# Attention's VectorE steps of the routing and of the x update in other periods, two TensorE jobs exchanged at attention's end, and one GpSimd power moved in the MLP

## The reference

```python
x = x + attn_a(layernorm(x))     # 16 heads of 64, causal softmax, output matrix W_O
x = x + ffn(layernorm(x))        # mixture of experts
x = x + attn_b(layernorm(x))     # linear attention, 8 heads, and a gated MLP
x = x + ffn(layernorm(x))        # the same mixture of experts again
```

```python
def attn_a(x):                                   # per row of x and head
    scores = tril(k @ q.T) - 1e10 * (1 - mask)
    attn = softmax(scores / 8)
    z = attn @ v;   return z_flat @ W_O.T
def ffn(x):                                      # x is normalised a second time inside
    xn = (x - mu) * rsqrt(var + eps) * gamma + beta
    probs = softmax(xn @ Wr + br)                # 8 experts
    scores, idx = top_k(probs, 2)
    full = relu(xn @ W1[e] + b1[e]) @ W2[e] + b2[e]
    return x + sum(scores * (full[idx] - c[idx] + c.sum()))
```

## Time and profile before

| | |
|---|---|
| median of 3 runs | 1351.04 us (1348.25 to 1354.89) |
| profiled execution, time | 1348.61 us |
| profiled execution, span | 1346.7 us |
| TensorE busy | 1208.7 us (90%) |
| VectorE busy | 912.4 us (68%) |
| ScalarE busy | 829.2 us (62%) |
| GpSimd busy | 505.1 us (38%) |
| attention's rows 1 to 7 | about 78 to 524 us |

### The profile page before, as it was taken

One profiled execution on the slowest core, in us unless ns is written; L12 is line 12 of the kernel. 1 busy time (PEld: TensorE's weight loads), 2 busy tenths in 40 slices (PEclk: granted clock), 3 DMA queues, 4 the chain that ended last, 5 costly groups with the idle time before them and its releaser, 6 DMA issues. The chain is left out here.

```text
span 1346.7 us, 26854 instructions
## 1 busy us (share of the span) xinstructions
PE 1208.7 (90%) x7787; PEld 917.0 (68%) x7787; DVE 912.4 (68%) x3538; ACT 829.2 (62%) x2478; POOL 505.1 (38%) x619
## 2 busy tenths in 40 slices
PE   6999999999999998799985999999996988199990
PEld 5666666666666665599973777777774656199990
DVE  6788888887878785444436888888873667234445
ACT  6898888888888886144432555656554665044440
POOL 2111324142414131545541344433432376545550
PEclk9999999999999999799996999999997999599995
DMA  9100000000000000222221000000000011222226
GB/s 291 49 2 1 12 7 11 7 13 6 16 7 13 5 13 1 72 69 71 69 64 62 17 16 17 17 1 1 1 1 0 15 39 40 76 59 73 69 71 195
DMA packets 54442, 52.89 MB, mean 39 GB/s; under 512 B 7341, under 2 KB 43098, under 8 KB 54330
## 3 DMA queue, kind: packets, MB, share of 16 engines
q1 hardware_dynamic: 36320, 29.39, 7.7%
q0 software_dynamic: 8928, 17.84, 3.9%
q10 hardware_dynamic: 9082, 4.33, 1.1%
HBM read 29.48 MB, written 22.05 MB: 38 GB/s over the span
## 5 line engine op out<-in xcount | busy, mean ns | idle before, releaser
L1354 ACT ACTIVATE prob<-prob,negmax 128x256 f32<-128x256 f32 (+3 forms) x512 | 283.2, 556 | 47.6 <-DVE negmax L1448 47.5
L1448 DVE CUSTOM_DVE_ANT_0 prob<-bank,mask 128x256 f32<-128x256 f32 (+3 forms) x512 | 223.9, 480 | 41.9 <-PE bank L1164 41.6
L1524 POOL TENSOR_TENSOR Vs<-Vh_sb,rinv 128x512 f32<-128x512 f32 x64 | 66.6, 1041 | 365.7 <-DVE rinv L1426 365.7
L1050 POOL DMA_INDIRECT expert_out<-f_x_yb,f_x_to x142 | 136.7, 963 | 153.0 <-DVE f_x_yb L1038 118.3
L1176 PE MATMUL bank<-prob,Vs 128*64 128x512 f32 (+3 forms) x1024 | 152.0, 439 | 0.5 <-POOL Vs L1524 0.4
L678 POOL DMA_INDIRECT expert_in<-f_xn,f_slot x128 | 126.9, 991 | 49.1 <-issue 31.2
L982 PE MATMUL bank<-f_x_xbT,W_sb 128*128 128x256 f32 x568 | 138.3, 387 | 1.7 <-DVE f_x_xbT L1018 1.7
L1003 ACT ACTIVATE f_x_hid<-bank,cols 128x256 f32<-128x256 f32 x144 | 63.8, 474 | 92.1 <-PE bank L982 92.1
L982 PEld LDWEIGHTS bank<-f_x_xbT,W_sb 128*128 128x128 f32 x568 | 104.6, 194 | 14.8 <-DVE f_x_xbT L1018 2.9
L1003 ACT ACTIVATE prob<-bank,cols 128x256 f32<-128x256 f32 x140 | 62.0, 473 | 79.6 <-PE bank L982 79.6
L1176 PEld LDWEIGHTS bank<-prob,Vs 128*64 128x64 f32 x1024 | 63.6, 136 | 69.7 <-issue 60.0
(11 more groups left out here) (263 smaller groups left out, 3181.2 us busy)
## 6 DMA issues: line engine op xcount, KB each, us to landing
f_x_xb<-expert_in SPq DMA_DIRECT2D x73, 130.0 KB, 2.2
b_crows<-expert_out SPq DMA_DIRECT2D x16, 256.0 KB, 2.7
c_crows<-expert_out SPq DMA_DIRECT2D x16, 256.0 KB, 4.2
expert_out<-f_x_yb,f_x_to POOLq DMA_INDIRECT x142, 2.5
expert_in<-fill ACTq DMA_DIRECT2D x16, 130.0 KB, 2.5
x_sb<-in_L_attn_a_x_dram SPq DMA_DIRECT2D x8, 256.0 KB, 6.7
W_sb<-in_L_ffn_W_dram SPq DMA_DIRECT2D x1, 2048.0 KB, 10.2
expert_in<-f_xn,f_slot POOLq DMA_INDIRECT x128, 2.3
```

Of the source, the lines that this page charges most:

```text
L1050: pool.indirect_dma_start(yg, bass.IndirectOffsetOnAxis(ap=self.to[:, t:t + 1], axis=0), self.yb[:, t, :], None).then_inc(self.stored[t], 16)
L1354: nc.scalar.activation(mine, mine, ACT.Exp, scale=-1.0, bias=negmax[:, g % 2, i, a:a + 1], accum_out=rowsum[:, g % 2, i, a:a + 1]).then_in ...
L1448: nc.vector.tensor_tensor_reduce(out=prob[:, g % 2, a, columns(i)], in0=score_bank(i, a), in1=mask[:, T - width[i]:], scale=-1.0, scalar=H ...
```

## The change

Four edits; the number of instructions on every engine stays the same.

1. The x update in place leaves `dve_normalise`, becomes `dve_update`, and in attention's rows comes behind P4 instead of behind P3. It also waits for the normalised tiles.
2. `dve_top` and `dve_topid` of the routing go from behind P6 to inside P6, after mask j = 5. The five later steps stay behind P6.
3. At attention's end `PV` of pair 7 comes ahead of `out_of` of pair 6.
4. At the MLP's end the power of row 7 comes ahead of all scatters of row 6.

```diff
-                if self.in_place and not self.lean:
-                    self.wait_rstd(dve, b, update=True)
-                    for t in range(NT):
-                        tile = self.src[:, bass.ds(b * NT + t, 1), :]
-                        nc.vector.tensor_scalar(tile, tile, self.power[:, u, 6, t:t + 1], self.power[:, u, 7, t:t + 1],
-                                                ALU.mult, ALU.subtract).then_inc(self.y, 1)
+
+            def dve_update(self, dve, b, u):
+                self.wait_rstd(dve, b, update=True)
+                dve.wait_ge(self.xn, START + b * NT + NT)
+                for t in range(NT):
...
-            ROUTE_DVE = {5: (route.dve_logit, route.dve_rmax, route.dve_shift),
-                         6: (route.dve_top, route.dve_topid, route.dve_ids,
-                             route.dve_is_k, route.dve_sel, route.dve_row_sel),
-                         7: (route.dve_place, route.dve_picked, route.dve_slotf, route.dve_slots)}
+            ROUTE_DVE_INSIDE = {5: (route.dve_logit,), 6: (route.dve_top, route.dve_topid), 7: (route.dve_place,)}
+            ROUTE_DVE_BEHIND = {5: (route.dve_rmax, route.dve_shift),
+                                6: (route.dve_ids, route.dve_is_k, route.dve_sel, route.dve_row_sel),
+                                7: (route.dve_picked, route.dve_slotf, route.dve_slots)}
...
+                    PV(B - 1, PAIRS - 1)
                     out_of(B - 1, PAIRS - 2)
-                    PV(B - 1, PAIRS - 1)
                     out_of(B - 1, PAIRS - 1)
...
-                                    if g in (ROUTE_LOGITS, ROUTE_RANK) and not first:
-                                        ROUTE_DVE[g][0](dve, b - 1, 1 - u)
+                                    if not first:
+                                        for part in ROUTE_DVE_INSIDE.get(g, ()):
+                                            part(dve, b - 1, 1 - u)
...
-                                for part in ROUTE_DVE.get(g, ()):
-                                    if part not in (route.dve_logit, route.dve_place):
-                                        part(dve, b - 1, 1 - u)
+                                if g == ROUTE_TR:
+                                    route.norm.dve_update(dve, b - 1, 1 - u)
+                                for part in ROUTE_DVE_BEHIND.get(g, ()):
+                                    part(dve, b - 1, 1 - u)
...
                     route.dve_normalise(dve, B - 1, 1)
+                    route.norm.dve_update(dve, B - 1, 1)
...
-                        route.pool_scatter(pool, LAST - 1, slot_of(LAST - 1), 0, 2)
                         route.norm.pool_power(pool, LAST, slot_of(LAST))
-                        route.pool_scatter(pool, LAST - 1, slot_of(LAST - 1), 2)
+                        route.pool_scatter(pool, LAST - 1, slot_of(LAST - 1))
                         route.pool_scatter(pool, LAST, slot_of(LAST))
```

More of the change, by code:

```diff
@@ L405, in dve_normalise @@
                                             ALU.subtract, ALU.mult).then_inc(self.xn, 1)
-                if self.in_place and not self.lean:
-                    self.wait_rstd(dve, b, update=True)
-                    for t in range(NT):
-                        tile = self.src[:, bass.ds(b * NT + t, 1), :]
-                        nc.vector.tensor_scalar(tile, tile, self.power[:, u, 6, t:t + 1], self.power[:, u, 7, t:t + 1],
-                                                ALU.mult, ALU.subtract).then_inc(self.y, 1)
+            def dve_update(self, dve, b, u):
+                self.wait_rstd(dve, b, update=True)
+                dve.wait_ge(self.xn, START + b * NT + NT)
+                for t in range(NT):
+                    tile = self.src[:, bass.ds(b * NT + t, 1), :]
+                    nc.vector.tensor_scalar(tile, tile, self.power[:, u, 6, t:t + 1], self.power[:, u, 7, t:t + 1],
+                                            ALU.mult, ALU.subtract).then_inc(self.y, 1)
             def pool_finish(self, pool, b, u):
@@ L1500, in _ @@
                     route.dve_normalise(dve, B - 1, 1)
-                    for g in ROUTE_DVE:
-                        for part in ROUTE_DVE[g]:
+                    route.norm.dve_update(dve, B - 1, 1)
+                    for g in ROUTE_DVE_INSIDE:
+                        for part in (*ROUTE_DVE_INSIDE[g], *ROUTE_DVE_BEHIND[g]):
                             part(dve, B - 1, 1)
```

## The result

| | before | after |
|---|---|---|
| median | 1351.72 us of 4 runs (1348.25 to 1354.89) | 1339.03 us of 4 runs (1338.33 to 1340.33) |
| ratio to before, 95% interval | | 0.9898 [0.9869, 0.9928] |
| profiled execution, time | 1348.61 us | 1339.15 us |
| profiled execution, span | 1346.7 us | 1336.8 us |

A forecast was written before the change was run, and what follows sets the result against it. TensorE, busy most of the span, was taken to bound the kernel, losing time to VectorE's late first masks. Terms -4.2 - 5.3 + 0.8 - 1.5 = -10.2 us gave a median of 1340.8 us, range 1335 to 1347.

The forecast's parts named there:

- The reading: Attention's P4 and P7: a late first mask on VectorE delays TensorE's small job beyond 2.92 us by the same amount.
- P4, -4.2: Moving the x update behind P4 gives back 0.62 us in six rows and 0.53 in the last: 4.2 us.
- P5's room, 0.14 us: The moved 1.02 us update fits VectorE's 1.16 us wait ahead of P5's first mask, with 0.14 us to spare.
- P7, -5.3: Moving part of the selection inside P6 lets P7's first mask start earlier: 3.4 to 5.7 us back, 5.3 taken.
- The worst case (0.27 us late): P7's first mask, after a late K_lo and five remaining steps, still starts 0.27 us late instead of 0.82.
- PV in front, +0.8: Attention's end: the exchange makes one TensorE rest of 2.8 us; range -0.5 to +1.5 us, +0.8 taken.
- The +1.5: Attention's end: if the clock falls inside PV, the statistics and all 16 scatters wait 1.5 us longer; sum then -9.5.
- The last power, -1.5: MLP's end: the power starts 1.5 us earlier, and row 7's slots and scatters follow 1.5 us earlier.
- The K_lo wait: Rival: K_lo of P6 becomes 1.23 us late and delays P7, so P7 returns nothing: 1346.1 us, chance 0.14.
- The clock did not stay up: Rival at attention's end: the clock stays up in PV, -0.5 instead of +0.8: 1339.5 us, chance 0.27.
- VectorE's wait ahead of P5 is no free time: Rival: moved work is paid wherever put, P5 7.1 and P6 8.6 us: +5.8 in all, 1356.8 us, chance 0.04.
- The change did what it says: Opposed rival: attention's waits are really ScalarE's pace and periods stay as long; 1350.3 us, chance 0.07.

The follow-up runs named there:

- edits 2, 3 and 4 alone: Three kernels, each the kernel before with only edit 2, only edit 3 or only edit 4: 1345.13, 1352.64 and 1350.59 us.
- edit 3 alone: The kernel before with only PV of pair 7 put ahead of out_of of pair 6 at attention's end: 1352.64 us, ratio 0.9997.
- edit 4 alone: The kernel before with only the MLP's last power put ahead of all scatters of row 6: 1350.59 us, ratio 0.9991.
- the rest filled: Changed kernel with ten unread matmuls in TensorE's rest ahead of the last value product: 1338.91 us; with due work there and six scatters moved earlier: 1336.04 us.
- the kernel with two sums: The changed kernel with two unused VectorE sums over 128x512 behind the x update in P4: 1352.2 us, ratio 0.9999.
- edit 1 alone: The kernel before with only the x update moved from behind P3 to behind P4: 1348.97 us, ratio 0.9967.
- the doses: The changed kernel with two, then one, unused VectorE sums over 128x512 behind the x update in P4: 1352.2 and 1340.98 us.
- one sum: The changed kernel with one unused VectorE sum over 128x512 behind the x update in P4: 1340.98 us, ratio 0.9914.

## Why the prediction was right, point by point

- **The reading.** Lateness of a first mask passes to TensorE one for one: shown. With the lateness gone the small jobs stand at 2.92 us, and put back by 0.37 and 0.95 us with idle VectorE work it comes back at that size.
- **P4, -4.2.** Measured -3.9 (4.23 to 0.31). The 0.25 us that are left are all in row 1, whose small job stands at 3.17 or 3.18 in every kernel with edit 1 while its mask is on time; the stall of before covered whatever it is.
- **P5's room, 0.14 us.** Measured 0.24 (1.19 us of sums, 0.95 us late). The update starts ahead of K_lo's listed end (117.37 against 116.76 + 0.69), which I had not counted.
- **P7, -5.3.** Measured -6.1: the term was too small. The worst case (0.27 us late) did not occur: in row 1 the moved piece takes 1.12 us from its first step (130.03) to mask j = 6 (131.15), not 1.23, since the cast's own wait is not in it, and K_lo was never late. The prediction also said that the five rows between lay like the first and the last; row 5's P7 lost 1.18 us. In that row VectorE was idle for 0.31 us ahead of P7's first mask, which started 1.99 us after the scores instead of 1.62 to 1.64. The extra 0.36 us stands in row 5 of the kernels with edits 2, 3 and 4 alone too, in none with edit 1; its cause is open.
- **PV in front, +0.8.** Measured +0.6 at the experts' first matmul, in the changed kernel and with edit 3 alone, each against the one profile of before. That the number came out is partly luck: with the same old order at attention's end the first matmul stands at 40.73 to 40.82 us in three profiles, at 42.74 with edit 4 alone and at 39.36 in the changed kernel without the exchange, and with the exchange at 39.66 to 41.59 in five, so one pair can't size this term. The mechanism held in the changed kernel. Taken apart: the rest is 2.81 us, as forecast 2.8; the clock falls 0.55 us into the product (a mean of 0.75 over 1.10 us is 0.55 us at full and 0.55 at half rate), where I had 0.85, and the product loses 1.67 instead of 1.5 us; the later fall stays away (16 transposes 1.97 us instead of 3.41) and gives most of it back. The Trainium skill's rule (TensorE: Matmul & The Clock Gate, section Why this matters for your kernels) says that idle gaps between bursts of matmuls bring the clock back to half rate; the page has gaps somewhat longer than this one in mind. The trace agrees with the rule for the product of the changed kernel (4.05 us, and 2.38 with the rest filled) and not for that of the kernel with two sums (2.37 us behind the same rest). The +1.5 that I set beside that rule is nearer to what the exchange costs inside the changed kernel (2.1 us) than my +0.8.
- **The last power, -1.5.** Measured -1.46, and row 7's first scatter is just free when its slots come (0.46 us of wait where 0.30 is GpSimd's own pause), as worked out.
- **Sum.** -10.2 forecast; the four terms as measured add to -10.9, and the stretches that the edits touch to -10.4, since the changed kernel started row 1 0.43 us later. The profiled times differ by 9.5, the medians by 12.7 (1339.03 against 1340.8 forecast), and where the medians' further 2 us come from is not shown; -10.2 lies inside the interval of 9.7 to 17.7. P7's missing 0.8 us and P4's surplus of 0.3 are the larger of the errors.
- **The rivals.** The K_lo wait did not appear, but it is real: behind 0.2 us of room it comes, and 1.26 us more of work inside P6 made the period 1.08 us longer. The clock did not stay up in the product of the changed kernel; it did in the kernel with two sums. The prediction counted for that rival that a rest of 1.57 us in the last row had cost nothing; with edit 1 alone the same wait (1.58 us) was followed by a fall, with the clock at 1.2 GHz from 516.9 to 520.3 and pair 6's product at 3.38 us instead of 2.37. That VectorE's wait ahead of P5 is no free time is refuted by the doses: 0.24 us of it are still free. The change did what it says.

## What to carry to other kernels

Compare the same job's distance from the start of its period in periods with and without extra work: the difference is what the work costs, and the wait of the engine in the neighbouring period is the room to move it to. The room ends where a later product of the same engine becomes due, so look for it on both sides of the moved piece. An exchange that merges two rests of TensorE into one can cost more than the work it hides; with the rest filled, idly or with work that is due anyway, the product ran at full clock in both profiles. And where the clock can fall, one pair of profiles doesn't size an edit: look at the same place in every kernel that leaves it alone.

## What was not expected of the hardware

TensorE's clock fell inside attention for rests far shorter than 2.8 us. With two sums behind the update, TensorE rested 0.42 us ahead of the value projection and 0.31 us ahead of the router's logits (eight columns each, 1.06 us), stayed busy otherwise, and in rows 5 to 7 the granted clock went to 0.50 for 3.4 us, so that P5 took 10.9 us, while rows 1 to 4, with the same rests, kept it at 1.00 and took 9.34 to 9.37 us. With one sum it fell in no row. So a stall of 0.95 us can cost 2.5, and not in each period: the times of the kernel with two sums spread over 14.5 us in 12 runs, those of the changed kernel over 2 in 4.
